# Attention with a mixture of experts on one core: the expert slot in another order, and the key copies of the first half between the exponentials

## The chip, the core and the metric

The kernel runs on one core of a Trainium2 chip. The core has a matrix engine (TensorE, PE in the rows; its weight loads are PEld), VectorE (DVE), ScalarE (ACT), GpSimd (POOL) and SyncE (SP), which here only issues DMAs. Each engine works through its own list of instructions in order and waits on semaphores that the others raise. The metric is the device time of one execution in microseconds, the median of the runs.

## What is computed

The input is 16 sequences of 512 rows with 128 features, 8192 rows in all. The rows are normalised, and three things are added: the row itself, the output of an attention block, and that of a layer of experts.

```
xn   = layernorm(x)
# attention, 16 heads of 64
h    = rmsnorm(xn) * norm_scale
q, k, v = h @ wq, h @ wk, h @ wv
w    = softmax(q k^T / 8)          # 512 x 512 for each sequence and head
a    = (w v) @ w_out + b_out
# experts: 8, of which each row uses 2
logit = silu(xn @ rw1 + rb1) @ rw2 + rb2
p, e  = softmax(top2(logit)), index
f     = sum over the 2 experts:  p * (silu(xn @ w1[e] + b1[e]) @ w2[e] + b2[e])
out  = x + a + f
```

## The kernel before

**Attention in ticks.** The attention is 64 units: a unit is one sequence, one half of its queries (256) and four pairs of heads. A unit has four ticks, `G` counts them from 0 to 255, and `k = G % 4` is the tick's place in its unit. In every tick PE makes two steps of scores (L313) into the two first pairs of PSUM banks, DVE takes the maxima of both (L555), ACT makes the exponentials (`PR`, L911) and DVE turns them (`PT`, L563). In ticks with k = 0 and 1 PE also multiplies the weights of the previous unit with the values (L332). At k = 2 DVE divides by the denominators (`OT`, L572), PE makes the queries of the next unit (L298) and the output projection (L345), and DVE adds the projection to `acc` (L595 or L598) after its second transpose. At k = 3 PE makes keys (L283 to L286) and values (L271), and ACT copies them to SBUF (`KS` L884, `V` L918). A new group of keys is needed first by the tick after one with G % 8 = 7.

**Two halves.** In ticks 0 to 127 the router also runs: it decides for each row the two experts and scatters the rows to a table in HBM that is sorted by expert. From tick 139 on the experts run, in 39 blocks of 512 rows (`NT`).

**The expert slot.** `SLOTS` holds the tick of each block: every tick with k = 2 from 142 on (29 of them), and every twelfth from 139 on, which has k = 3 (139, 151, 163 and so on to 247, ten of them). So nine slots with k = 3 follow right behind one with k = 2, and 20 with k = 2 stand alone. In the slot of block i, behind the attention's work of that tick, stand in the order of the list `PLAN[G]`: the *turn* of the rows of block i+1 (PE transposes them, L239 of `XG`; ACT and DVE split them into a high and a low part `X2`, L983 and L800), the *second product* of block i-1 (`expert_out`, PE L472; DVE scales and adds the bias, `give_back`, L813 and L817, to `YS`), and the *first product* of block i in four quarters (`expert_in`, PE L222 to L224). For each quarter ACT makes tanh (`ZT`, L995) and a biased copy (`HH`, L997), which frees the quarter's PSUM bank, and DVE multiplies the two (`halves`, L806). Quarters 0 and 1 of `halves` stand in the slot, quarters 2 and 3 in the next tick behind its maxima (the list `LATE`). Every engine reads the same `PLAN`, so an order in it is an order on PE, ACT and DVE alike. `give_back` ends in four indirect DMAs that POOL issues (`back`, L1174).

**PSUM banks.** Banks 0 to 3 hold scores. Banks 4 to 7 go around as a ring (`Ring`): each new product takes the next, and before it writes waits until the previous user of that bank has been read (`came_free`). The ring starts at bank 4 in each tick with k = 2. For a slot at such a tick the output projection's bank is the one just before the slot's first bank, and it is free when DVE has made `acc`.

**Key copies.** ACT's exponentials of a tick are two calls of `probs`. `alone(G)` says whether both copies of keys stand between them. Before, it holds in the second half alone, for ticks with G % 8 = 7 without a slot; in the first half one copy stands between them and one behind.

## Time and profile before

| | |
|---|---|
| median of 3 runs | 1888.17 us (1884.29 to 1891.51) |
| profiled execution | 1887.85 us, span 1886.0 us |
| PE busy | 1817.7 us, 96% of the span |
| DVE busy | 1625.3 us, 86% |
| ACT busy | 1209.1 us, 64% |
| granted TensorE clock | 0.997 |
| DMA | 130.15 MB, mean 69 GB/s |

The span is from the first instruction to the last of the profiled execution. A busy share says how long an engine had an instruction under way, not that it limits the kernel: each engine waits at some place of a tick for another, and the tick's length is set by the chain of such waits. The length of a tick is read as the distance between the first maxima (L555) of that tick and of the next. A row of a window has its limits, its length, then the busy time of PE, PEld, DVE, ACT and POOL in it (with the number of instructions), the granted TensorE clock, the busy share of the DMA engines and GB/s.

### The profile page before, as it was taken

To read this page: it belongs to the slowest core of one execution; us is meant where nothing else is said; L and a number is where in the kernel's file an instruction comes from. 1 tells how busy PE (TensorE), PEld (TensorE's weight loads), DVE (VectorE), ACT (ScalarE), POOL (GpSimd) and SP (SyncE) were. 2 spreads that over 40 slices of the span, in tenths; PEclk is the share of its full clock that TensorE was granted. 3 is DMA by queue.
4 is the path that set the end of the run, shared out by engine and by line. 5 is a ranking of instruction groups with operands and counts; after the bars stand their busy time and mean duration, and the time that the engine had idled before them with its cause. 6 is when DMAs were issued, how large, how long until landed. Compare 5 with 4: busy or idle time off the path is not lost.

```text
span 1886.0 us, 74660 instructions
## 1 busy us (share of the span) xinstructions
PE 1817.7 (96%) x32554; PEld 1177.0 (62%) x32554; DVE 1625.3 (86%) x2297; ACT 1209.1 (64%) x2987; POOL 733.0 (39%) x641
## 2 busy tenths in 40 slices
PE   8999999999999999998999999999999999999997
PEld 5555555555555555554567766767676667666765
DVE  6999999999999999989888888788888888888886
ACT  6666776666666666664666675666676666666663
POOL 4244655444544445432023334324324333333143
PEclk9999999999999999999999999999999999999999
DMA  3033321111111111111433434333433333333333
GB/s 96 22 83 109 101 95 52 42 48 37 48 37 48 48 48 46 30 40 56 110 74 78 90 73 90 78 84 78 89 74 66 92 65 87 76 84 78 79 74 56
DMA packets 154487, 130.15 MB, mean 69 GB/s; under 512 B 27664, under 2 KB 139024, under 8 KB 154128
## 3 DMA queue, kind: packets, MB, share of 16 engines
q1 hardware_dynamic: 123568, 104.65, 20.3%
q0 software_dynamic: 30592, 20.73, 8.1%
q8 instruction: 255, 4.18, 0.9%
q14 instruction: 72, 0.59, 0.1%
HBM read 93.15 MB, written 34.27 MB: 68 GB/s over the span
## 4 chain that ended last, share of the span: by engine, by line
PE 40%; ACT 28%; DVE 18%; issue 12%; DMA 1%; POOL 0%; POOLq 0%; SPq 0%; ACTq 0%; DVEq 0%
ACT PR L911 18%; PE pair L332 11%; DVE NM L555 8%; PE pair L472 8%; PE pair L313 7%; DVE PT L563 4%; PE pair L345 3%; ACT ZT L995 3%; ACT HH L997 3%; PE pair L298 3%; DVE OT L572 3%; ACT KS L884 1%; PE pair L239 1%; PE pair L388 1%; PE pair L271 1%
## 5 line engine op out<-in xcount | busy, mean ns | idle before, releaser
L911 ACT ACTIVATE PR<-pair,NM 128x512 f32<-128x512 f32 x1024 | 696.3, 697 | 536.9 <-DVE NM L555 536.4
L563 DVE STREAM_TRANSPOSE PT<-PR 128x1024 f32<-128x1024 f32 x512 | 633.2, 1241 | 119.2 <-ACT PR L911 105.7
L555 DVE TENSOR_REDUCE NM<-pair 128x2 f32<-128x1024 f32 x512 | 598.0, 1208 | 19.6 <-PE pair L313 18.9
L313 PE MATMUL pair<-KS,QS 64*32 64x512 f32 x8192 | 505.3, 598 | 16.6 <-ACT PR L911 9.3
L332 PE MATMUL pair<-PT,V 32*64 32x256 f32 x16384 | 479.7, 378 | 17.9 <-ACT HH L997 9.7
L332 PEld LDWEIGHTS pair<-PT,V 32*64 32x64 f32 x16384 | 383.6, 131 | 166.6 <-issue 107.3
L1174 POOL DMA_INDIRECT out<-YS,IDW x156 | 248.4, 1592 | 536.8 <-DVE YS L817 334.3
L313 PEld LDWEIGHTS pair<-KS,QS 64*32 64x32 f32 x8192 | 122.7, 106 | 261.7 <-issue 157.4
L911 ACT ACTIVATION_READ_ACCUMULATOR PR<-pair,NM 128x1 f32 x1024 | 218.9, 214 | 0.0
L995 ACT ACTIVATE ZT<-pair,BT 128x512 f32<-128x512 f32 x156 | 109.8, 704 | 108.1 <-PE pair L224 108.0
L1132 POOL DMA_INDIRECT slots<-XR,IDX x128 | 124.4, 972 | 73.9 <-issue 38.5
L472 PE MATMUL pair<-E,HH 128*128 128x128 f32 x1248 | 148.1, 277 | 2.9 <-DVE HH L806 2.9
L472 PEld LDWEIGHTS pair<-E,HH 128*128 128x128 f32 x1248 | 144.1, 194 | 4.4 <-DVE HH L806 3.8
L806 DVE SCALAR_TENSOR_TENSOR HH<-ZT,HH 128x512 f32<-128x512 f32 x156 | 104.1, 688 | 43.6 <-ACT HH L997 43.6
L298 PE MATMUL pair<-HF,WQ 128*128 128x256 f32 x512 | 126.1, 389 | 10.1 <-DVE OT L572 9.3
L298 PEld LDWEIGHTS pair<-HF,WQ 128*128 128x128 f32 x512 | 92.1, 190 | 62.2 <-DVE OT L572 49.5
L1121 POOL TENSOR_TENSOR TH<-TH,HS 128x512 f32<-128x512 f32 x64 | 82.1, 1282 | 120.1 <-ACT HS L951 120.1
L345 PE MATMUL pair<-OT,WO 128*128 128x256 f32 x512 | 123.6, 384 | 2.2 <-DVE OT L572 2.2
L271 PE MATMUL pair<-WV,HF 128*32 128x128 f32 x4096 | 125.1, 274 | 0.0
L271 PEld LDWEIGHTS pair<-WV,HF 128*32 128x32 f32 x4096 | 107.8, 110 | 23.4 <-issue 23.3
L345 PEld LDWEIGHTS pair<-OT,WO 128*128 128x128 f32 x512 | 94.7, 190 | 37.7 <-issue 9.5
L997 ACT ACTIVATE HH<-pair,BT 128x512 f32<-128x512 f32 x156 | 110.4, 708 | 0.0
(129 smaller groups left out, 1798.1 us busy)
## 6 DMA issues: line engine op xcount, KB each, us to landing
RB<-l_rows SPq DMA_DIRECT2D x128, 256.0 KB, 4.3
E<-w_tab SPq DMA_DIRECT2D x39, 512.0 KB
XG<-slots SPq DMA_DIRECT2D x39, 264.0 KB, 4.0
E<-in_w SPq DMA_DIRECT2D x39, 256.0 KB, 3.9
xin<-in_x SPq DMA_DIRECT2D x16, 256.0 KB, 2.8
XQ<-in_x SPq DMA_DIRECT2D x16, 256.0 KB, 3.1
l_rows<-RT SPq DMA_DIRECT2D x256, 2.0 KB
w_tab<-SPL SPq DMA_DIRECT2D x8, 512.0 KB, 2.6
```

Source lines behind the costliest of these rows:

```text
L271: m = pe.do.matmul(bank[bk][32 * a:32 * a + 32, j * P:j * P + P], HF[:, keys], WV[:, pair], start=True, stop=True, tile_position=(0, 32 * a))
L298: m = pe.do.matmul(bank[bk][:, 256 * i:256 * i + 256], WQ[:, pair], HF[:, 256 * half:256 * half + 256], start=True, stop=True)
L313: m = pe.do.matmul(bank[2 * (s % 2) + r][32 * c:32 * c + 32, :], QS[rows, u % 2, c, at:at + 32], KS[rows, g % 2, c, :], start=True, stop=T ...
L332: m = pe.do.matmul(bank[GH + a][DH * c:DH * c + DH, 0:256], V4[rows, g % 2, k, DH * c:DH * c + DH], moving, start=(k == 0), stop=(k == 15) ...
L345: m = pe.do.matmul(bank[bk][:, 0:256], WO[:, GH * (u // 2 % 2) + a, :], OT[:, a, :], start=(a == 0), stop=(a == GH - 1))
L472: m = pe.do.matmul(bank[bk][:, t * P:(t + 1) * P], HH[:, i % 2, c, t * P:(t + 1) * P], E2[:, i % 2, c * P:(c + 1) * P], start=(c == 0), st ...
L555: dve.do.tensor_reduce(NM[:, step % 4], pairs[s % 2][:], AX.X, ALU.max, negate=True).then_inc(sem["dve_max"])
L563: dve.do.transpose(PT[:].rearrange("p c k q -> p (c k) q")[:, :, 32 * slot:32 * slot + 32], PR[:, step % PRB].rearrange("p r k -> p (r k)" ...
L911: act.do.activation(PR[:, step % PRB, r, :], bank[2 * (s % 2) + r], ACT.Exp, bias=NM[:, step % 4, r:r + 1], accum_out=RS[:, g % 2, r, at:a ...
L995: act.do.activation(ZT[:, n % 2], ps, ACT.Tanh, bias=BT[:, i % 3, 8 + c:9 + c], scale=0.5).then_inc(sem["act_zt"])
L997: act.do.activation(HH[:, i % 2, c], ps, ACT.Identity, bias=BT[:, i % 3, c:c + 1]).then_inc(sem["act_zz"])
L1174: pool.do.indirect_dma_start(out, bass.IndirectOffsetOnAxis(ap=IDW[:, i % 4, t, 0:1].bitcast(U32), axis=0), YS[:, i % 2, t, :], None, comp ...
```

## The change

In `PLAN` a slot now holds the first product's four quarters, then the turn of the next block's rows, then the second product of the block before and its `back`. All four quarters of `halves` stand in the slot, and `LATE` is gone. `alone` holds for every tick with G % 8 = 7 that has no slot, so in the 16 such ticks of the first half both copies of keys stand between the two calls of `probs`; in the second half the places of the key copies are the same as before.

```diff
--- before.py
+++ after.py
@@ -191,17 +191,13 @@
 
         SLOTS = sorted([FIRST + 12 * k for k in range(NT - (UNITS - FIRST // 4 - 1))] + [4 * u + 2 for u in range(FIRST // 4 + 1, UNITS)])
         PLAN = {G: [] for G in range(TIMES + 8)}
-        LATE = {G: [] for G in range(TIMES + 8)}
         PLAN[FIRST - 1].append((0, "turn"))
         for i, G in enumerate(SLOTS):
+            PLAN[G] += [(i, "h", c) for c in range(NC)]
             if i + 1 < NT:
                 PLAN[G].append((i + 1, "turn"))
             if i:
-                PLAN[G].append((i - 1, "y"))
-            PLAN[G] += [(i, "h", c) for c in range(NC)]
-            LATE[G + 1] += [(i, c) for c in (2, 3)]
-            if i:
-                PLAN[G].append((i - 1, "back"))
+                PLAN[G] += [(i - 1, "y"), (i - 1, "back")]
         PLAN[TIMES - 1].append((NT - 1, "y"))
         PLAN[TIMES].append((NT - 1, "back"))
 
@@ -825,7 +821,7 @@
                         rows_low(i)
                     if what == "y":
                         give_back(i)
-                    if what == "h" and c[0] < 2:
+                    if what == "h":
                         halves(i, c[0])
 
             dve.do.memset(junk[:], 0.5).then_inc(sem["dve_junk"])
@@ -850,8 +846,6 @@
                     maxima(u, 2 * k + 1)
                 attending(G)
                 between(G)
-                for i, c in LATE[G]:
-                    halves(i, c)
                 if u < UNITS:
                     turn_probs(u, 2 * k)
                     if G % 8 == 2 and 0 < G // 8 <= NB:
@@ -895,7 +889,7 @@
                 act.do.copy(XT[:], bank[BANK["xT", r]]).then_inc(sem["act_xTs"])
 
             def alone(G):
-                return G >= 8 * NB and G % 8 == 7 and G not in SLOTS
+                return G % 8 == 7 and G not in SLOTS
 
             def probs(g, s):
                 step = STEPS * g + s
@@ -928,7 +922,7 @@
                 u, k = divmod(G, 4)
                 g, first = u // 2 + 1, u % 2 * 2
                 if k == 3 and g < 2 * NB:
-                    if G >= 8 * NB and not alone(G):
+                    if G in SLOTS or G % 8 == 3 and G >= 8 * NB:
                         keys(g, first)
                     if not alone(G):
                         keys(g, first + 1)
```

On PE, the slot of tick 194 before (from the projection's last matmuls on; `XG` are the rows that are turned, `E2,HH` the second product, `X2,E1` the first product, in brackets the semaphores waited for):

```order
L345 MATMUL pair3<-OT,WO 128x256 x3
L239 MATMUL pair3<-idn,XG 128x128 [waits s_rows_1]
L239 MATMUL pair3<-idn,XG 128x128 x3
L472 MATMUL pair2<-E2,HH 128x128 [waits s_act_q,s_e2_1,s_dve_s]
L472 MATMUL pair2<-E2,HH 128x128 x15
L222 MATMUL pair2<-X2,E1 128x512 [waits s_act_q,s_e1_0]
L223 MATMUL pair2<-X2,E1 128x512
L224 MATMUL pair2<-X2,E1 128x512
L222 MATMUL pair3<-X2,E1 128x512 [waits s_dve_acc]
```

And of the same slot of the changed kernel its last part, from the fourth quarter of the first product on (quarters one to three stand ahead of it, behind the projection, and wait for `s_e1_0` and `s_act_q`):

```order
L218 MATMUL pair3<-X2,E1 128x512 [waits s_dve_acc]
L219 MATMUL pair3<-X2,E1 128x512
L220 MATMUL pair3<-X2,E1 128x512
L235 MATMUL pair3<-idn,XG 128x128 [waits s_act_zz,s_rows_1]
L235 MATMUL pair3<-idn,XG 128x128 x3
L468 MATMUL pair2<-E2,HH 128x128 [waits s_act_zz,s_e2_1,s_dve_s]
L468 MATMUL pair2<-E2,HH 128x128 x15
L309 MATMUL pair0<-KS,QS 32x512 [waits s_act_exp]
```

The wait for `acc` was at the second quarter, after turn and second product; it is now at the fourth, ahead of both, and the second product is the slot's last work on PE. The lines are four lower because the diff takes lines away.

On DVE, the same slot and the tick after it, before (`HH<-ZT,HH` are the quarters, `X<-pair,X` the turn's low part, `NM` the maxima):

```order
L598 TENSOR_TENSOR acc<-pair,acc 128x256
L800 TENSOR_TENSOR X<-pair,X 128x512
L813 SCALAR_TENSOR_TENSOR YS<-pair,B 128x512
L817 TENSOR_TENSOR YS<-YS,IDW 128x512
L806 SCALAR_TENSOR_TENSOR HH<-ZT,HH 128x512 x2
L555 TENSOR_REDUCE NM<-pair 128x2 x2
L806 SCALAR_TENSOR_TENSOR HH<-ZT,HH 128x512 x2
L563 STREAM_TRANSPOSE PT<-PR 128x32x32 x2
```

And there in the changed kernel:

```order
L594 TENSOR_TENSOR acc<-pair,acc 128x256
L802 SCALAR_TENSOR_TENSOR HH<-ZT,HH 128x512 x4
L796 TENSOR_TENSOR X<-pair,X 128x512
L809 SCALAR_TENSOR_TENSOR YS<-pair,B 128x512
L813 TENSOR_TENSOR YS<-YS,IDW 128x512
L551 TENSOR_REDUCE NM<-pair 128x2 x2
L559 STREAM_TRANSPOSE PT<-PR 128x32x32 x2
```

All four quarters now stand ahead of the next tick's maxima, and so do, right before them, the two operations on the second product.

On ACT, a tick of the first half with G % 8 = 7 before:

```order
L911 ACTIVATE PR,RS<-pair,NM 128x512 x2
L884 COPY KS<-pair 128x512
L911 ACTIVATE PR,RS<-pair,NM 128x512 x2
L884 COPY KS<-pair 128x512
L918 COPY V<-pair 128x512 x2
L895 COPY XT<-pair 128x512
```

And the same tick of the changed kernel:

```order
L905 ACTIVATE PR,RS<-pair,NM 128x512 x2
L878 COPY KS<-pair 128x512 x2
L905 ACTIVATE PR,RS<-pair,NM 128x512 x2
L912 COPY V<-pair 128x512 x2
L889 COPY XT<-pair 128x512
```

The second copy of keys has moved from behind the tick's last exponentials to ahead of them.

## Rows read from the trace of the kernel before

**Rows 1.** The page: the chain that ended last, by engine

```profile
PE 40%; ACT 28%; DVE 18%; issue 12%; DMA 1%; POOL 0%; POOLq 0%; SPq 0%; ACTq 0%; DVEq 0%
```

**Rows 2.** Waits: who waited for whom, us in total, times, longest

```profile
ACT ZT L995 <- PE pair L224: 108.0, 38, 3.7
```

**Rows 3.** Timeline of DVE, tick 194: start, length, instruction, [idle before, releaser]

```profile
1366.91 2.34 DVE L555 TENSOR_REDUCE NM<-pair 128x2 f32<-128x1024 f32 x2
...
1373.11 0.39 DVE L598 TENSOR_TENSOR acc<-pair,acc 128x256 f32<-128x256 f32 x1
...
1374.21 0.69 DVE L813 SCALAR_TENSOR_TENSOR YS<-pair,B 128x512 f32<-128x512 f32 x1
...
1378.09 2.35 DVE L555 TENSOR_REDUCE NM<-pair 128x2 f32<-128x1024 f32 x2
1380.36 1.28 DVE L806 SCALAR_TENSOR_TENSOR HH<-ZT,HH 128x512 f32<-128x512 f32 x2
```

**Rows 4.** Timeline of PE, tick 194

```profile
1370.00 0.60 PE L239 MATMUL pair<-idn,XG 128*128 128x128 f32 x4
1370.44 3.74 PE L472 MATMUL pair<-E,HH 128*128 128x128 f32 x32
1373.93 0.48 PE L222 MATMUL pair<-X,E 128*128 128x512 f32 x1
...
1376.89 1.95 PE L313 MATMUL pair<-KS,QS 64*32 64x512 f32 x32
```

**Rows 5.** Timeline of ACT, tick 194: first and last of the eight on the quarters

```profile
1374.91 0.69 ACT L995 ACTIVATE ZT<-pair,BT 128x512 f32<-128x512 f32 x1 [2.52 <-PE pair L224]
...
1378.91 0.73 ACT L997 ACTIVATE HH<-pair,BT 128x512 f32<-128x512 f32 x1
```

**Rows 6.** Windows of ticks 186, 190, 195, 191, 135, 187 and 188

```profile
1299.47:1311.07 11.60, 11.60 (x92) 9.62 (x98) 9.07 (x12) 7.93 (x18) 3.26 (x4) 1.00 0.09 24
1337.11:1348.54 11.43, 11.43 (x88) 9.44 (x95) 8.48 (x11) 7.43 (x17) 6.42 (x5) 1.00 0.68 146
1378.09:1384.23 6.14, 6.10 (x118) 3.22 (x102) 6.11 (x10) 6.14 (x15) 4.80 (x4) 1.00 0.41 37
1348.54:1355.32 6.78, 6.58 (x126) 3.34 (x118) 6.22 (x9) 6.16 (x15) 5.68 (x4) 1.00 0.33 31
900.88:907.47 6.59, 5.49 (x110) 2.89 (x116) 5.10 (x8) 4.72 (x12) 0.00 (x0) 1.00 0.93 209
1311.07:1324.52 13.45, 12.81 (x166) 9.39 (x150) 9.60 (x15) 10.23 (x23) 4.77 (x4) 1.00 0.48 105
1324.52:1330.69 6.17, 5.22 (x160) 3.74 (x160) 5.79 (x8) 3.97 (x11) 0.00 (x0) 1.00 0.03 5
```

**Rows 7.** Window of tick 192, which has no expert work

```profile
1384.23:1389.43 5.20, 5.07 (x160) 3.75 (x160) 4.72 (x5) 2.82 (x9) 0.00 (x0) 1.00 0.11 18
```

**Rows 8.** Timeline, first half, ticks 84 to 90: DVE, ACT and PE

```profile
569.44 2.36 DVE L555 TENSOR_REDUCE NM<-pair 128x2 f32<-128x1024 f32 x2 [0.52 <-PE pair L313]
...
586.98 1.25 DVE L563 STREAM_TRANSPOSE PT<-PR 128x1024 f32<-128x1024 f32 x1 [0.58 <-ACT PR L911]
...
586.82 0.60 ACT L884 COPY KS<-pair 128x512 f32<-128x512 f32 x1
587.29 1.11 ACT L918 COPY V<-pair 128x512 f32<-128x512 f32 x2
...
587.48 1.95 PE L313 MATMUL pair<-KS,QS 64*32 64x512 f32 x32 [0.20 <-ACT KS L884]
...
600.88 1.99 PE L298 MATMUL pair<-HF,WQ 128*128 128x256 f32 x8 [0.41 <-DVE OT L572]
```

**Rows 9.** Granted clock and idle PE: tick 139, the last tick, its second product

```profile
930.87 0.63 PE L239 MATMUL pair<-idn,XG 128*128 128x128 f32 x4 [1.81 <-ACT KS L884]
...
1863.54 5.46 PE L472 MATMUL pair<-E,HH 128*128 128x128 f32 x32 [2.86 <-DVE HH L806]
...
1863.50:1869.00 5.50, 5.46 (x32) 5.27 (x32) 2.61 (x4) 0.67 (x3) 1.55 (x1) 0.69 0.28 25
```

## The prediction, made before the changed kernel was run

> **What bounds the kernel now.** I read the chain that ended last first: it changes between three engines, PE 40%, ACT 28%, DVE 18% [rows 1], so no engine is the limit by itself and the time has to be worked out tick by tick. The list of waits then names what looks wasteful in a slot: ACT waits 108.0 us in all for the first product, 38 times, 2.8 us each [rows 2]. The windows show what kinds of tick there are. A tick without expert work takes 5.20 us with DVE busy for 4.72 and PE for 5.07 [rows 7]; slots at k = 2 take 11.43 and 11.60 [rows 6] and, by its two first maxima, tick 194 takes 1378.09 - 1366.91 = 11.18 [rows 3]. The timelines of DVE, PE and ACT in tick 194 show the slot's own chain. PE ends the second product and goes over to the first at 1373.93, hands over the first quarter, and ACT, which was free 2.52 us earlier, starts at 1374.91 [rows 4, 5]. DVE multiplies two quarters and is at the next maxima at 1378.09 [rows 3]. The bound of a slot is thus PE until its first quarter, then ACT, then DVE. What matters in the changed order is which of these the next maxima stand behind.
>
> **The slot at k = 2, 29 times.** Nothing is computed more or less; it is all order. After the projection PE is at the slot's work at 1370.00, 3.09 us after the first maxima of the tick [rows 3, 4]. Now the first product comes first. It takes 1376.89 - 1373.93 = 2.96 us, 0.74 a quarter [rows 4]. Its banks go on in the ring from the projection's: the fourth quarter has the projection's own bank and waits for DVE's `acc`, as the order's wait says. `acc` stands behind DVE's second transpose, which the change doesn't touch, and ends at 1373.11 + 0.39 = 1373.50, 6.59 us into the tick [rows 3]. Without that wait the quarter would start at 3.09 + 3 x 0.74 = 5.31; so PE stands idle for 1.3 us. Before, it used this bank after turn and second product, when `acc` was long made.
>
> From there on the chain has no gap: 0.06 us for the semaphore (an estimate: from DVE's first `OT`, half of a pair, to PE's start at 600.88 it is no more [rows 8]), 0.74 for the quarter, 1370.44 - 1370.00 = 0.44 for the turn, and from the second product's start to DVE's read of it 1374.21 - 1370.44 = 3.77 [rows 3, 4]. The two waits for ACT's reads of quarters one and two don't bind: ACT was free at 1374.91 - 2.52 = 1372.39 even behind the turn's copy of 0.6, so its first quarter starts at about 4.9 us; it needs (1378.91 + 0.57 - 1374.91) / 4 = 1.14 us for each [rows 5] and has read the second at 7.2, while PE gets to the second product at 6.59 + 0.06 + 0.74 + 0.44 = 7.83. Then DVE has `give_back`, two operations of 0.69 [rows 3], and only behind them the next maxima. Sum: 7.83 + 3.77 + 1.38 = 12.98, say 13.0. Against tick 194 that is +1.8, against 190 +1.55, against 186 +1.4 [rows 3, 6]. The fourth kind (G % 16 = 6) is put with 186. The mean is 1.54; ticks that were already longer for reasons of their own lose less, so I take 1.5. The last slot, tick 254, is counted with the end; 28 x 1.5 = +42.0 us.
>
> How low could it be? If `acc` came so early that PE didn't wait, the second product would still wait for ACT's second quarter (7.2), so 7.2 + 3.77 + 1.38 = 12.35. And ACT and DVE alone give no less: four quarters end on ACT at 4.9 + 4.56 = 9.5, DVE's fourth at 10.2, its low part after the turn at 10.9, `give_back` 12.3. Below: 28 x (12.35 - 11.46) = +25. ACT's wait of 2.8 us does go, but all that ACT gains stays in front of DVE's in-order queue, which now waits for PE's last work in the slot.
>
> **The tick after a slot.** It gives back the two quarters of `halves`, 1.28 us on DVE between maxima and transposes [rows 3]. Where tick k = 3 is G % 8 = 3 and no slot, DVE filled it (6.11 of 6.14 busy [rows 6]). Without the quarters it is like a bare tick, 5.20, with 0.4 for the denominators at the unit's end (an estimate: 6.14 less maxima of 2.3, quarters of 1.2 and two transposes of 1.15 [rows 3, 6, 8]): 5.6, so -0.55, not -1.28, because DVE then waits for the exponentials. Ten times: -5.5. Where G % 8 = 7, ACT sets the length: 6.78 in tick 191 against 6.59 in tick 135, the same work without a slot before it [rows 6], so -0.2, ten times: -2.0.
>
> **The slot at k = 3, nine times behind another and once, tick 139, by itself.** Its first quarter's bank is that of a key copy. ACT starts half a pair of maxima into the tick, 1.2, and has 4.72 of exponentials and copies, as in tick 135 [rows 3, 6]; that makes 5.9. Its second quarter is read at 5.9 + 2 x 1.14 + 0.1 = 8.3; PE's second product starts there and is read at 8.3 + 3.77 = 12.1, `give_back` ends at 13.4, and 0.4 of denominators make 13.85. Before: 13.45 [rows 6]. So +0.4, and the tick after goes from 6.17 to a bare 5.20 [rows 6, 7], -0.97. Together 9 x -0.57 = -5.1. Tick 139 has no second product before it and now waits for four quarters and the turn instead of two: about +2.2 - 0.96 = +1.2.
>
> **The key copy of the first half, 16 ticks.** The copy takes 587.29 - 586.82 = 0.47 us of ACT [rows 8]. Moved ahead of the tick's last exponentials it delays these, and DVE already waited 0.58 for them before its transpose at 586.98. In return PE loses a wait of 0.20 for the copy at 587.48. Who is late next? DVE's chain runs on from here until PE waits 0.41 for its `OT` at 600.88, and DVE in turn waits for PE at the tick after a k = 3 (0.52 at 569.44) [rows 8]. So the transpose is on the path and PE's 0.20 is not: 16 x 0.47 = +7.5. If PE were the path it would be -3; I keep both ends and take +7.5, since the waits on either side name DVE.
>
> **The end.** In the last tick the second product waited 2.86 us for the late quarters [rows 9]; now it does not. DVE reads it behind its transposes in any case, so this gives back tick 254's own loss of about 2.4 and some more: -1 for both.
>
> **DMA and POOL.** SP and POOL have the same list as before. Rows and weights for the next block are fetched in the slot ahead, `YS` is ready later by 5 us, and POOL has no work close behind it. Nothing.
>
> **Sum.** 42.0 - 5.5 - 2.0 - 5.1 + 1.2 + 7.5 - 1.0 = +37.1. The profiled execution took 1887.85 us, its span 1886.0; the median of the runs, 1888.17, is 0.3 above it. 1887.85 + 37.1 = 1924.95, so 1925.
>
> **The clock.** Tick 139 shows PE idle for 1.81 us with the granted clock at 1.00 in the ticks around it [rows 6, 9]; the idle of 2.86 us before the last second product was followed by 0.69, between the levels of 1.2 and 2.4 GHz, and 5.46 us for it instead of 3.74 [rows 4, 9]. The new wait is 1.3 us, so I cost it at nothing. The Trainium skill speaks against this: "TensorE: Matmul & The Clock Gate", section "A second HAM failure mode: psum-queue depth-cycling", tells of a kernel whose PE, going through PSUM banks in turn, had small idle gaps between groups and swung between the two clocks. By that rule the time would be that of the third rival below; the trace, with waits for banks of up to 1.81 us at 1.00, does not agree so far.
>
> **Rivals.**
> 1. *No wait for `acc`.* Another reader of the bank order could say that DVE's `acc` will come earlier once DVE has no late quarters. For it: the queue before `acc` is shorter only in ticks at k = 3. Against it: `acc` follows the second transpose of its own tick, which ACT sets. Slot 12.35: 1888 + 37 - 28 x 0.65 = 1907. Chance 0.07.
> 2. *PE is the bound and has no new wait: not slower.* Place: the fourth quarter. For it: PE is busy for 5.07 of 5.20 in a bare tick [rows 7], so ticks behind a slot could repay a late start if PE ran ahead. Then DVE's 1.5 would vanish, and PE's waits around the slots at k = 3 would go (13.45 - 12.81 = 0.64 and 6.17 - 5.22 = 0.95 [rows 6], nine times -14), with +7.5 from the first half: 1888 - 7 = 1881. It decides if PE waits under 0.3 us for the fourth quarter. Against it: DVE reaches each next maxima last in rows 3. Chance 0.03.
> 3. *The clock falls in the slots.* 1.7 us more for the second product in 28 slots, +48: 1972. Chance 0.04.
> 4. *The change is only half of this:* the key copy costs nothing or gains 3: 1914 to 1917. That lies inside my range and has no chance of its own.
>
> **Numbers.** The forecast of 1925, with its own range of 1912 to 1934, has 0.83; rival 1 0.07, rival 2 0.03, rival 3 0.04, and 0.03 remain for a time within the noise. The range of 1908 to 1937 leaves out rival 2, rival 3 and part of rival 1. About 0.5% is what a measurement of this kernel can tell from no change. Faster by more than that 0.02, within it 0.04, slower 0.94.
>
> **What would show it.** Ticks at k = 2 with a slot of about 13.0 us, the last wait in them DVE's for the second product (L809, from PE L468); a PE wait of 1.3 us for `acc` before the fourth quarter (L218 from DVE L594 or L591), 28 times; ACT's wait for PE before ZT gone; ticks behind lone slots of 5.6 and 6.6; 7.8 in the first half where 7.3 was. I am wrong if slots at k = 2 stay under 12 us, or if the ticks without expert work change.

## The result and the profile after

| | before | changed |
|---|---|---|
| median of 4 runs | 1889.25 us (1884.29 to 1891.51) | 1939.08 us (1938.28 to 1940.4) |
| profiled execution, span | 1887.85, 1886.0 us | 1938.28, 1936.5 us |
| PE busy, DVE busy, ACT busy | 1817.7, 1625.3, 1209.1 us | 1830.9, 1644.2, 1208.8 us |
| granted TensorE clock | 0.997 | 0.997 |

The changed kernel is slower: 1.0268 times the time before, with an interval of 1.0246 to 1.029. The forecast was 1925 with a range up to 1937, so the direction held and the size did not: +50 where +37 was forecast. Beside e1 to e8 the kernel before took about 1888 us; in e9 to e15 every kernel, the one before too, took some 8% longer (the last section shows where in the tick order), and those are compared among themselves, or in ticks that are the same in both.

The page, the chain that ended last by engine; DVE has gone from 18% to 30% of it, and PE from 40% to 20% [rows 1]:

```profile
ACT 32%; DVE 30%; PE 20%; issue 15%; DMA 2%; POOL 0%; SPq 0%; POOLq 0%; ACTq 0%; DVEq 0%
```

The waits of the changed kernel (us in total, times, longest):

```profile
PE pair L218 <- DVE acc L594: 18.6, 15, 1.4
...
PE pair L218 <- DVE acc L591: 12.4, 14, 1.3
...
ACT ZT L989 <- DVE HH L802: 2.5, 4, 1.1
```

PE now waits for `acc` 15 + 14 = 29 times, once in each slot at k = 2. ACT's 108.0 us behind the first product [rows 2] are gone.

The slot of tick 178 (first maxima 1264.54) on DVE, then on PE, then on ACT: start, length, instruction, [idle before, releaser]:

```profile
1264.54 2.34 DVE L551 TENSOR_REDUCE NM<-pair 128x2 f32<-128x1024 f32 x2
...
1270.74 0.39 DVE L594 TENSOR_TENSOR acc<-pair,acc 128x256 f32<-128x256 f32 x1
...
1274.34 0.69 DVE L802 SCALAR_TENSOR_TENSOR HH<-ZT,HH 128x512 f32<-128x512 f32 x1 [0.46 <-ACT HH L991]
...
1276.20 0.69 DVE L809 SCALAR_TENSOR_TENSOR YS<-pair,B 128x512 f32<-128x512 f32 x1 [0.57 <-PE pair L468]
1276.92 0.69 DVE L813 TENSOR_TENSOR YS<-YS,IDW 128x512 f32<-128x512 f32 x1
1277.53 2.35 DVE L551 TENSOR_REDUCE NM<-pair 128x2 f32<-128x1024 f32 x2
```

```profile
1271.18 0.50 PE L218 MATMUL pair<-X,E 128*128 128x512 f32 x1 [1.29 <-DVE acc L594]
...
1272.42 3.74 PE L468 MATMUL pair<-E,HH 128*128 128x128 f32 x32
```

```profile
1269.40 0.72 ACT L989 ACTIVATE ZT<-pair,BT 128x512 f32<-128x512 f32 x1
...
1278.79 0.69 ACT L905 ACTIVATE PR<-pair,NM 128x512 f32<-128x512 f32 x1 [4.07 <-DVE NM L551]
```

Set against [rows 3 to 5]: ACT starts the quarters 4.86 us into the tick instead of 8.00, and then stands idle for 4.07 us before the next exponentials. PE stands 1.29 us at the fourth quarter, its second product starts at 7.88, DVE reads it at 11.66 and is at the next maxima at 12.99. The chain of the prediction is in these rows link by link.

Windows of ticks 186, 187, 188 and 195 of the changed kernel (columns as in [rows 6]), and of tick 175:

```profile
1326.08:1339.24 13.16, 12.25 (x100) 9.74 (x98) 10.43 (x15) 9.37 (x20) 1.92 (x2) 1.00 0.13 29
1339.24:1353.28 14.04, 13.06 (x166) 9.56 (x150) 9.89 (x15) 9.83 (x21) 6.69 (x5) 1.00 0.45 102
1353.28:1358.48 5.20, 5.20 (x168) 3.35 (x160) 4.72 (x6) 2.78 (x8) 0.00 (x0) 1.00 0.03 5
1408.99:1414.61 5.62, 5.62 (x118) 3.22 (x102) 5.11 (x8) 4.37 (x12) 4.65 (x3) 1.00 0.27 26
1237.81:1252.96 15.15, 14.06 (x199) 10.49 (x191) 11.91 (x14) 10.05 (x21) 8.84 (x7) 1.00 0.44 94
```

They were 11.60, 13.45, 6.17 and 6.14 [rows 6]; tick 175 was 13.44. In the first half, tick 87 of the changed kernel, ACT and then DVE and PE, where [rows 8] have the copy of keys at the transpose:

```profile
594.55 0.71 ACT L905 ACTIVATE PR<-pair,NM 128x512 f32<-128x512 f32 x1
...
595.22 1.10 ACT L912 COPY V<-pair 128x512 f32<-128x512 f32 x2
```

```profile
595.39 1.25 DVE L559 STREAM_TRANSPOSE PT<-PR 128x1024 f32<-128x1024 f32 x1 [1.07 <-ACT PR L905]
```

```profile
595.14 1.95 PE L309 MATMUL pair<-KS,QS 64*32 64x512 f32 x32
```

DVE's wait for the exponentials has grown from 0.58 to 1.07, and PE's 0.20 for the copy is gone. The tick is 7.80 instead of 7.32.

**All ticks, sorted by kind**, each measured from first maxima to first maxima in the two profiled executions:

| ticks | count | before | after | difference in sum | forecast |
|---|---|---|---|---|---|
| slots at k = 2, without 254 | 28 | 11.56 | 13.02 | +42.36 | +42.0 |
| after lone slots, G % 8 = 3 | 10 | 6.14 | 5.62 | -5.24 | -5.5 |
| after lone slots, G % 8 = 7 (the tenth is tick 255, counted with the end) | 9 | 6.79 | 6.59 | -1.80 | -2.0 |
| slots at k = 3 and the ticks after | 9 + 9 | 13.44, 6.17 | 14.04 (two 15.15), 5.20 | -1.7 | -5.1 |
| tick 139 and the one after | 2 | 9.92, 6.17 | 12.32, 5.20 | +1.4 | +1.2 |
| first half, G % 8 = 7 | 16 | 7.32 | 7.80 | +7.52 | +7.5 |
| first half, all others | 112 | 6.42 | 6.42 | +5.97 | 0 |
| tick 254 and all behind it | | 9.60 | 11.58 | +2.9 | -1.0 |
| the rest and the start | | | | -1.0 | 0 |

Before and after are medians. The sum is +50.5, as the spans say. What the forecast missed is +6.0 in ticks of the first half that the change doesn't touch, +3.9 at the end and +3.4 at the slots with k = 3.

**Where VectorE stands still.** The extra time of the first half lies in four ticks: 33 (+2.09), 34 (+1.28), 41 (+0.99) and 90 (+2.37), together 6.7; small differences in the others take 0.8 off. In three of the four a VectorE operation is much longer than usual; tick 34 has another cause, shown further down. Tick 33 of the changed kernel, on DVE and on POOL:

```profile
233.61 2.64 DVE L669 SCALAR_TENSOR_TENSOR gt<-gt,CON 128x32 f32<-128x32 f32 x1
```

```profile
233.91 1.29 POOL L1153 TENSOR_TENSOR SPL<-RAW,SPL 128x512 fp32r<-128x512 f32 x1
235.15 1.04 POOL L1059 TENSOR_TENSOR HR<-xin,mv 128x512 f32<-128x512 f32 x1
236.27 1.04 POOL L1062 TENSOR_TENSOR HR<-HR,sqo 128x512 f32<-128x512 f32 x1
```

An operation on 128 x 32 elements took 2.64 us, where the same line takes 0.17 in other ticks, and it ended at 236.25, 0.06 us behind the second of two GpSimd operations. In tick 175 the quarters of `halves` do the same, DVE and then POOL:

```profile
1245.05 4.21 DVE L802 SCALAR_TENSOR_TENSOR HH<-ZT,HH 128x512 f32<-128x512 f32 x3 [1.93 <-ACT HH L991]
```

```profile
1244.91 1.64 POOL L1059 TENSOR_TENSOR HR<-xin,mv 128x512 f32<-128x512 f32 x1
1246.62 1.38 POOL L1062 TENSOR_TENSOR HR<-HR,sqo 128x512 f32<-128x512 f32 x1
```

Taken apart, the first quarter lasts 2.05 us and the second 1.52 instead of 0.69. Over the whole profiled execution, ten DVE operations were over 0.4 us longer than the median of their line, 12.4 us beyond it in all, and GpSimd had a TENSOR_TENSOR under way beside each; before, there were two such, 2.3 us beyond it, both in tick 127.

**Tick 34.** No operation on VectorE is stretched in it. PE, which had waited for the stretched chain of tick 33, ran its next products at a lower granted clock (PE, then the window):

```profile
239.38 3.04 PE L294 MATMUL pair<-HF,WQ 128*128 128x256 f32 x8 [2.55 <-DVE OT L568]
```

```profile
239.40:242.20 2.80, 2.80 (x8) 2.30 (x9) 2.80 (x4) 1.11 (x3) 0.00 (x0) 0.64 0.00 0
```

In e1, which has the same stretched operation in tick 33, PE waits 2.40 us there, the clock stays at 1.00, the same eight matmuls take 1.99 us and tick 34 is 6.51 as before. So +1.28 of the +6.0 is the clock's. That it fell because of the longer wait is likely and not shown.

**The end.** POOL's first and last additions of the last two blocks, before:

```profile
1857.76 1.55 POOL L1174 DMA_INDIRECT out<-YS,IDW  x1 [16.12 <-DVE YS L817]
...
1876.47 1.55 POOL L1174 DMA_INDIRECT out<-YS,IDW  x1 [0.30 <-issue]
```

And in the changed kernel, with the last product of PE and DVE's last operation:

```profile
1909.87 1.55 POOL L1168 DMA_INDIRECT out<-YS,IDW  x1 [21.62 <-DVE YS L813]
...
1926.99 1.55 POOL L1168 DMA_INDIRECT out<-YS,IDW  x1 [0.30 <-issue]
```

```profile
1909.94 3.84 PE L468 MATMUL pair<-E,HH 128*128 128x128 f32 x32
1915.94 8.85 PE L328 MATMUL pair<-PT,V 32*64 32x256 f32 x256 [2.15 <-DVE YS L809]
```

```profile
1933.03 0.69 DVE L611 TENSOR_TENSOR xin<-pair,xin 128x512 f32<-128x512 f32 x1 [4.25 <-DMA xin<-out]
```

The last second product is no longer late (3.84 us and no wait, against 5.46 and 2.86 [rows 9]). But counted from the last tick's first maxima (1859.93 and 1909.51) the last addition starts at 17.48 instead of 16.54 us, and the end waits for the output that is read behind these additions. The chain that ended last, in order of time (start, length, step), says what the second group of additions waited for:

```profile
1915.42 4.51 DMA out<-YS,IDW
```

VectorE had the last `YS` ready at 1916.52, but the second group starts only at 1921.44, behind the landing of the first group's last addition. Before, the second group started at 1870.92, 0.46 us behind `YS`. The order moved the first group: it starts 0.36 us behind the last tick's first maxima, and before 2.17 us ahead of them.

### The profile page after: what moved, and what is told of

The parts are those of the page before. It is cut to its first block, busy times and chain, and to the rows that moved or that the text cites. A ratio compares the mean times of both kernels' runs of the same rounds, so it can differ in the third digit from the quotient of the medians.

```text
span 1936.5 us, 74661 instructions
## 1 busy us (share of the span) xinstructions
PE 1830.9 (95%) x32554; PEld 1179.4 (61%) x32554; DVE 1644.2 (85%) x2297; ACT 1208.8 (62%) x2987; POOL 734.2 (38%) x641
## 4 chain that ended last, share of the span: by engine, by line
ACT 32%; DVE 30%; PE 20%; issue 15%; DMA 2%; POOL 0%; SPq 0%; POOLq 0%; ACTq 0%; DVEq 0%
ACT PR L905 24%; DVE NM L551 13%; PE pair L468 7%; DVE PT L559 6%; PE pair L328 4%; DVE OT L568 4%; PE pair L309 3%; ACT QS L884 3%; ACT KS L878 2%; PE pair L384 1%; DVE YS L809 1%; ACT ZT L989 1%; ACT HH L991 1%; DVE YS L813 1%; ACT V L912 1%
## 5 line engine op out<-in xcount | busy, mean ns | idle before, releaser
L309 PE MATMUL pair<-KS,QS 64*32 64x512 f32 x8192 | 510.8, 597 | 19.4 <-ACT PR L905 16.7
L905 ACT ACTIVATION_READ_ACCUMULATOR PR<-pair,NM 128x1 f32 x1024 | 211.5, 207 | 0.0
L802 DVE SCALAR_TENSOR_TENSOR HH<-ZT,HH 128x512 f32<-128x512 f32 x156 | 111.8, 718 | 69.6 <-ACT HH L991 68.6
```

Of the source, the lines that this page charges most:

```text
L309: m = pe.do.matmul(bank[2 * (s % 2) + r][32 * c:32 * c + 32, :], QS[rows, u % 2, c, at:at + 32], KS[rows, g % 2, c, :], start=True, stop=T ...
L905: act.do.activation(PR[:, step % PRB, r, :], bank[2 * (s % 2) + r], ACT.Exp, bias=NM[:, step % 4, r:r + 1], accum_out=RS[:, g % 2, r, at:a ...
```

## The experiments

### e1_keys: the key copies alone

```diff
-                return G >= 8 * NB and G % 8 == 7 and G not in SLOTS
+                return G % 8 == 7 and G not in SLOTS
-                    if G >= 8 * NB and not alone(G):
+                    if G in SLOTS or G % 8 == 3 and G >= 8 * NB:
```

> Only the key copy of the first half is moved; the expert slots are as before. My theory: the 16 ticks with G % 8 = 7 take 7.8 us instead of 7.32 (the copy's 0.47 delays the exponentials, and DVE's transposes behind them), nothing else changes in them: 1889 + 7.5 = 1897. The changed kernel's first half had 6 us more than that, in ticks 33, 34, 41 and 90, where a tiny DVE operation took 1 to 2.6 us while POOL computed. If these come of the shifted times, they stand in this run too and it takes 1903; if they are chance, they are gone or elsewhere. Rival (PE was the path and loses its 0.2 us wait for the copy): 1886.

1897.76 us, ratio 1.0053 (1.0039 to 1.0067). The 16 ticks are 7.80, +7.50 together, and ticks 33 and 41 have their +2.09 and +1.00 again, with the same stretched operations. So this half costs 9.4 us: the copy itself, and collisions that it causes by moving everything behind it. Tick 34 is 6.51 and tick 90 is 7.21 here, as before: of the changed kernel's four long ticks, two (3.1 us) are seen in this second trace and two (3.6 us) in the changed kernel's alone.

### e2_slot: the slots alone

The changed kernel with `alone` as before.

> Only the slot is changed (order and quarters), the key copies are as before. My theory: the second half is tick by tick that of the changed kernel (slots at k = 2 13.0, slots at k = 3 14.0, two of them 15.1 if POOL meets DVE's quarters in the same places), the first half that of before: 1939 less 7.5 to 13.5, so 1926 to 1932. Rival (the two edits share a cost): under 1920.

1928.11 us, ratio 1.0209 (1.0194 to 1.0225). The slots at k = 2 give +42.50, those at k = 3 are 14.04 and in ticks 175 and 223 again 15.15. +39.8 and +9.4 make 49.2 of the 49.8: within the scatter of the runs the two halves add.

### e3_order and e4_quarters: the order alone, the quarters alone

e3 has the new `PLAN` and keeps `LATE`; e4 has the old `PLAN` and all four quarters in the slot:

```diff
-            LATE[G + 1] += [(i, c) for c in (2, 3)]
-                    if what == "h" and c[0] < 2:
+                    if what == "h":
```

> The slot in the new order, but quarters 2 and 3 on DVE stay in the next tick; key copies as before. My theory (the next maxima stand behind the second product's read, whatever DVE does before it): slots at k = 2 stay at 13.0 although two quarters have left them, and the ticks after a slot keep 6.14, 6.79 and 6.17, so it loses the 17 us that the quarters' place gave back: 1929 + 17 = 1946. Rival (the four quarters ahead of the maxima are the cost, the order is free or a gain): slots back near 11.5, in all 1885 to 1895.

> The old order of the slot, but all four quarters stand ahead of the next tick's maxima; key copies as before. My theory: the old order starts ACT's quarters 3.1 us later, so here the maxima wait for the fourth instead of the second quarter, 2 x 1.14 = 2.3 us: slots at k = 2 13.4 to 13.9, slots at k = 3 15.7, ticks after a slot 5.6, 6.6 and 5.2: 38 x 2.3 - 17 = +70, so 1959, worse than both edits together (1929). The two edits are then not additive: 1946 and 1959 alone, 1929 together. Rival (additive): order + quarters = slot.

e3 1934.97 us, ratio 1.025 (1.0235 to 1.0266): slots at k = 2 are 13.01, and the ticks behind lone ones take 6.15 and 6.59, those behind k = 3 5.72. e4 1968.34, ratio 1.0425 (1.0408 to 1.0441): slots at k = 2 are 13.69, at k = 3 17.15. The loss of the slot is thus that of the order. To have all quarters in it costs nothing there and gives back 0.5 us in the ticks behind it with G % 8 = 3 or behind k = 3; the 0.2 in those with G % 8 = 7 is the order's. Without the order the quarters cost more than the whole change, because they come last on DVE (e4, tick 194, the last quarter and the next maxima):

```profile
1414.62 0.69 DVE L805 SCALAR_TENSOR_TENSOR HH<-ZT,HH 128x512 f32<-128x512 f32 x1 [0.46 <-ACT HH L996]
1415.23 1.22 DVE L554 TENSOR_REDUCE NM<-pair 128x2 f32<-128x1024 f32 x1
```

The two edits don't add, as e4's expectation said: in the new order the quarters lie beside PE's second product. The totals missed by 11 us below and 9 us above. In e3 the place of the quarters is worth about 10 us and not 17 (see the ticks behind the slots). In e4 the slots at k = 3 take 17.15 and not 15.7, and that is the clock. Tick 187, PE, then a window in it:

```profile
1346.19 1.09 PE L238 MATMUL pair<-idn,XG 128*128 128x128 f32 x4 [2.69 <-ACT KS L883]
```

```profile
1346.10:1349.50 3.40, 3.31 (x16) 3.34 (x17) 1.44 (x2) 1.90 (x4) 0.00 (x0) 0.50 0.06 8
```

PE waits 2.7 us in each of the nine slots, for the copy of keys that frees the bank. In eight of them the granted clock then falls to 0.50 for a while and the slot takes 17.0 to 17.2; in tick 163 it stays at 1.00 behind the same wait, and the slot takes 15.56.

### e5_acc: acc ahead of the second transpose

e2 with the projection's addition one step earlier on DVE in slots:

```diff
+                    if k == 2 and G in SLOTS:
+                        project_out(u - 1)
-                if k == 2 and 0 < u <= UNITS:
+                if k == 2 and 0 < u <= UNITS and G not in SLOTS:
```

> The slot of the changed kernel with key copies as before (1928.1), and in slots at k = 2 DVE makes acc ahead of its second transpose, in the gap of 1.07 us in which it waits for the exponentials. My theory (PE waits 1.3 us for acc before the fourth quarter and the chain from there is without a gap): that wait goes, the second product next waits for ACT to read the second quarter, 7.3 us into the tick, and slots at k = 2 take 7.3 + 3.8 + 1.4 = 12.5 instead of 13.0: 28 x -0.55 = -15, so 1913. It also prices the wait: 1.3 us of idle PE is worth 0.55 of time. Rival (the wait for acc is the whole loss of the slot): 11.7 us, 1891. Rival (DVE's queue sets the slot, not PE): 13.0 still, 1928.

1918.62 us, ratio 1.0163 (1.0147 to 1.0178), 9.5 less than e2. Slots at k = 2 are 12.65 in 22 of 28. PE no longer waits for `acc` (tick 194, PE, first maxima 1380.11):

```profile
1385.75 0.39 PE L220 MATMUL pair<-X,E 128*128 128x512 f32 x1
1386.41 0.63 PE L235 MATMUL pair<-idn,XG 128*128 128x128 f32 x4 [0.28 <-ACT HH L993]
1387.57 3.70 PE L468 MATMUL pair<-E,HH 128*128 128x128 f32 x31 [0.53 <-ACT HH L993]
```

The wait for ACT takes its place, as forecast for this case (12.35; 12.5 in the expectation). So `acc` is the bound in these 22, and worth only 0.3 to 0.4 us of the 1.46 by which the slot grew. The six slots with G % 16 = 10 keep their 13.16: there the second product starts at 7.98 us without the wait for `acc` and at 7.97 with it (tick 186), since ACT frees its bank that late in either kernel. Over all 28 slots the gain is 8.1 us, where 15 were expected.

### e7_lateback: the second product read behind the next maxima

e2 with `give_back` moved on DVE to behind the next tick's maxima.

> The slot of the changed kernel with key copies as before (1928.1), and DVE reads the second product (both operations of give_back) behind the next tick's maxima instead of ahead of them. My theory (the maxima stand behind DVE's read of PE's last product): the maxima then wait only for PE's next scores, which stand behind that product: slots at k = 2 take 7.85 + 3.5 + 1.0 = 12.4, slots at k = 3 12.9; the tick after pays for the read, 6.1 to 6.6. Sum -15 - 10 + 5 + 9 = -11 or -12, so 1916: most of the loss stays, since PE's order keeps the next scores late. Rival (only DVE's order is at fault): slots at k = 2 fall to 11.5, 1890.

1956.7 us, ratio 1.0357 (1.0339 to 1.0376), where 1916 was expected. The slots did get shorter (12.77 and 13.38), but the ticks behind k = 3 take 7.94 to 10.8 instead of 5.2. Tick 188, PE and DVE:

```profile
1352.52 3.71 PE L328 MATMUL pair<-PT,V 32*64 32x256 f32 x128 [2.35 <-DVE YS L809]
```

```profile
1357.36 1.23 DVE L551 TENSOR_REDUCE NM<-pair 128x2 f32<-128x1024 f32 x1 [1.98 <-PE pair L309]
```

PE needs the second product's bank for the values of the next tick, and DVE waits for PE at the maxima behind it. In both places tried something waits for `give_back`: in the changed order PE ends the second product too late for either. I had not asked who needs the bank.

### e6_gate: GpSimd's normalisation behind the maxima

e2 with GpSimd's normalisation of rows, from shortly before the second half on, kept back until DVE's first maxima of its tick:

```diff
+                    if b >= EARLY:
+                        pool.wait_ge(sem["dve_max"], 2 * G + 1)
```

> The slot of the changed kernel with key copies as before (1928.1), and POOL's two large operations on the next sequence's rows (HR) wait, from tick 129 on, for the first maxima of their own tick, so that they can't run ahead into DVE's quarters in ticks 175 and 223. My theory (DVE's operation stands still while POOL's runs beside it): both ticks fall from 15.15 to 14.04, DVE's quarters in them from 2.05 and 1.52 to 0.69 us; -2.2 us, 1926. Rival (the indirect DMAs or the fetches beside them slow the quarters): they stay at 15.15.

One run, 1921.97 us, span 1920.2 against e2's 1927.1. Ticks 175 and 223 are 14.05 instead of 15.15, and tick 127 is 7.35 instead of 9.64, which had the two stretched operations of the kernel before. No DVE operation was stretched any more. The last of four indirect DMAs in tick 175 on POOL, and the second quarter, which had taken 1.52:

```profile
1228.62 1.56 POOL L1170 DMA_INDIRECT out<-YS,IDW  x1 [0.30 <-issue]
```

```profile
1231.06 0.69 DVE L802 SCALAR_TENSOR_TENSOR HH<-ZT,HH 128x512 f32<-128x512 f32 x1 [0.47 <-ACT HH L991]
```

The indirect DMA still stands beside the first quarter (1229.90, 0.69 us), so the rival falls. With this the two GpSimd operations on `HR` are shown as the cause of the two longer slots: they moved away, their amount unchanged, and the 2.2 us came back. The whole run is 6 us under e2's median; 2.3 more are tick 127, the rest is not explained, and it is one run.

### e10_apart and e13_two: the same for the first half

e1 with one wait more on GpSimd ahead of the subtraction (`SPL`), in every tick that has one (e10), and only in ticks 33 and 41 (e13):

```diff
+                    pool.wait_ge(sem["dve_tr"], 2 * G + 3)
```

```diff
+                    if G in (33, 41):
+                        pool.wait_ge(sem["dve_gate"], 15 * (G // 8 - 1) + 11)
```

> The key copies alone (1897.8 us, ticks 33 and 41 longer by 2.1 and 1.0 us than before), and POOL's subtraction for the expert weights' low part (SPL, eight times between ticks 26 and 40) waits until DVE has made the first transpose of the tick after the one it is written in. My theory (the shifted times bring DVE's tiny operation of ticks 33 and 41 beside POOL's subtraction, and it stands still until that ends): ticks 33 and 41 are back at 6.4, the 16 ticks stay at 7.80, in all 1894.7. Rival (the two ticks are long through the DMAs): they stay at 8.5 and 7.4.

> The kernel before with the key copies of the first half moved, and one wait more: in ticks 33 and 41 GpSimd's subtraction on the split weights (SPL) waits until VectorE has made its small code operation of that tick (L673), the one that stood stretched to 2.64 and 1.55 us beside it. Theory (the small operation stands still because of GpSimd's): tick 33 is 2.1 us and tick 41 1.0 us shorter than with the key copies alone, no small operation is longer than 0.3 us there, the other ticks stay, the time is about 3 us under that of the key copies alone. Rival (the stretch comes from something else, a late semaphore or the scatters under way on the same DMA queues): both operations stay stretched and both ticks stay as they were.

e10 2060.62 us beside 2040.39 for the kernel before: a miss. Ticks 27, 28, 31, 35, 36 and 39 grew by 1.3 to 5.4 us against the kernels beside it, and twelve operations were stretched that had not been, in other lines and ticks (27, 31, 35, 39), each beside a GpSimd TENSOR_TENSOR. What stands behind the waiting subtraction in GpSimd's list came later: the router's first multiplication of tick 27 at 213.33, and at 208.83 in e13. e13 2037.83 beside 2043.22, ticks 33 and 41 both 6.42, and no stretched operation in it. But in e9 to e15 ticks 32 and 40 take 9 to 11 us more in every kernel, which moves what runs beside what, and e15, without any of these waits, also has 6.42 in both. With the key copies and without the waits no kernel ran there. So neither tells the theory from its rival. The collisions of the first half are read from the traces (ticks 33 and 41: the same operations, the same ends, in two kernels; tick 90 in one), and not shown by taking them away.

### e14_waits: the changed kernel with both waits

> The changed kernel with two waits more on GpSimd: that one in ticks 33 and 41, and, for the normalisation of rows in the second half, one for VectorE's first maxima of the tick. Theory (the part of the loss that the prediction left out is VectorE standing still beside GpSimd): ticks 33, 41, 175 and 223 lose 2.1, 1.0, 1.1 and 1.1 us, tick 127 loses about 2, in all 6 to 8 us less than the changed kernel, so about 1.7 to 2.1% over the kernel before on the same chip; k = 2 slots stay at 13.0, k = 3 slots are 14.04 all. Rival (the slot at k = 3 is longer by itself, or the waits of GpSimd delay what VectorE needs from it): the time stays within 2 us of the changed kernel's.

2070.57 us beside 2043.22, and 2071.96 for e15. The slots of ticks 175 and 223 are 14.11, those of e15, without the waits, 15.16 and 15.14; no operation was stretched. That repeats e6. The ratio is 1.013 where 1.017 to 1.021 was expected, one run each. It can't be set against the changed kernel, which has no run beside these; and in e9 to e15 the old order's slots at k = 2 take 11.7 to 11.8 us and not 11.56, the new order's 13.02 as ever, so the order costs about 11 us less in them there.

### e11_end and e15_end: the last slot in the old order

One kernel, run twice: e2 with the second product ahead in the last slot, and its quarters 2 and 3 late.

> The slot of the changed kernel with key copies as before (1928.1), but the last slot, tick 254, in the old order and with its late quarters. My theory (the end is set by POOL's two groups of indirect adds, which begin when the last but one second product is read, and the new order reads it 4.5 us later in its tick): tick 254 falls from 11.58 to 9.6 and the tail behind the last maxima from +0.7 to 0 against before; -2.7, so 1925.4. Rival (the tail comes from the late quarters that keep the last product waiting, as my prediction had it, so the old order makes the end slower): 1929 or more.

> The changed slots, key copies as before, and the last slot (tick 254) in the old order with its two late quarters. Theory of the end (the loss there is the last slot's own new length plus GpSimd's later start with the last blocks' additions): tick 254 9.8 instead of 11.6 and the time behind the last maxima up by 0.2 instead of 0.8 us, as in an earlier run of this kernel; in all 2 to 2.5 us under the changed slots alone. Rival (the end is bound by the transfers of the last block whatever the order): tick 254 shrinks and the part behind the last maxima grows by as much.

2070.29 and 2071.96 us. Tick 254 is 9.80 and 9.83 instead of 11.58, so the growth of tick 254 is the order's. What lies behind it was +0.15 against the kernel before in one run and +0.93 in the other, and among e9 to e15 it varies as much between kernels with the old end (e12 +1.18, e13 +0.17), so these two runs don't settle the +0.88. The earlier traces say more. From the last tick's first maxima to the end the old slot takes 25.95 to 26.42 us (the kernel before, e1, e8) and the changed one 26.81 to 26.97 (the changed kernel, e2, e5, e6). And e4, with the old order but the quarters ahead, takes 24.82, -1.27: there `YS` is ready as early as in the changed kernel (7.01 us behind the last tick's first maxima, and 10.53 before), the first group of additions starts 4.45 us ahead of those maxima, and the second at once. In e3 the first group is as late as in the changed kernel, but its last addition lands in 3.15 us and not 4.51, and the whole takes 25.86. By these rows the late first group takes the gain away, and the longer landing (4.3 to 4.5 us in the four kernels with the changed end) makes the loss; why it is longer stays open.

### e12_gate: the wait of e6 in the kernel before

> The kernel before with nothing but POOL's two operations on the next sequence's rows held back from tick 129 on. My theory: tick 127 7.3 instead of 9.64, no DVE operation longer than its kind's median by over 0.4 us; -2.3, 1885.6. Rival: no change, 1887.9.

2039.41 us beside 2040.39 (2034.75 to 2044.82): no difference that one run can show. Its trace has no stretched operation, but tick 127 takes 12.37 us there, so the 7.3 of the expectation can't be tried.

### e8_hybrid and e9_both: the new order where it costs least

The kernel before, with the new order and all quarters only in the nine slots at k = 3 that follow another; e9 adds the wait of e6.

```diff
+            ahead = G % 4 == 3 and G > FIRST
+            if ahead:
+                PLAN[G] += [(i, "h", c) for c in range(NC)]
...
+            if not ahead:
+                PLAN[G] += [(i, "h", c) for c in range(NC)]
+                LATE[G + 1] += [(i, c) for c in (2, 3)]
```

> The kernel before, with the new slot order and all four quarters in nine slots only: those at k = 3 behind another slot, where the change cost 0.6 us and gave back 0.97 in the tick after. All others, and the key copies, as before. My theory: 9 x (0.6 - 0.97) = -3.3 us, 1885, at the edge of what five rounds can tell; by the profile nine ticks of 14.04 and 5.20 instead of 13.44 and 6.17, if POOL doesn't meet the quarters (nothing before these slots is later than in the kernel before). Rival (the gain in the tick after needs the new order in the slot ahead as well): nothing gained, 1888 to 1890.

> The kernel before with two changes: the new slot order in the nine slots at k = 3 behind another slot (1883.6 by itself), and POOL's two operations on the next sequence's rows held back, from tick 129 on, until the first maxima of their own tick. My theory (a DVE operation stands still while POOL's runs beside it, and in tick 127 this costs 2.3 us): tick 127 falls from 9.65 to 7.3, all else stays: 1881.3. Rival (tick 127 is long for another reason that hit the kernel with the wait by chance): 1883.6.

e8 1883.58 us (1881.17 to 1886.89, 11 runs) beside 1887.86: ratio 0.9979 (0.997 to 0.9988), a little faster than before. The nine slots are 14.24 (+7.22) and the ticks behind them 5.21 (-9.19 over nine). The slots were expected at 14.04. Tick 187, where DVE comes to the second product:

```profile
1320.26 0.69 DVE L817 SCALAR_TENSOR_TENSOR YS<-pair,B 128x512 f32<-128x512 f32 x1 [0.28 <-PE pair L476]
```

That accounts for 2.0 of the 4 us; the slots at k = 2, which it leaves alone, were 2.3 us shorter in the sum. e9 2036.02 (12 runs) beside 2040.39, ratio 0.998 (0.9969 to 0.9991), the same as e8's: the wait adds nothing that can be measured. The 2.3 us that were expected of tick 127 can't be tried there, since that tick takes over 12 us in all of e9 to e15 but one (11.99).

## Why the prediction was half right

- **The slot at k = 2**: right, 13.02 for 13.0, and for the reason given. 29 waits of up to 1.4 us for `acc`, then turn, second product, `give_back` on one chain (tick 178). e5 takes the wait away and gets 12.65 in 22 slots where the lower end said 12.35; in the other six ACT is as late as `acc`, which the prediction had ruled out for all. e3 shows that the order alone does it.
- **The tick after, lone slots**: right, 5.62 and 6.59 for 5.6 and 6.6.
- **The key copy**: right, 7.80 and +7.52. DVE's wait took on the copy's length, and PE's 0.20 was worth nothing.
- **The clock**: right for the slots, where it stayed at 1.00 with 29 idle times of up to 1.4 us on PE, so the third rival did not come true. But the reason was thin, and part of that is luck. It set 1.3 us against the 1.81 us of tick 139, behind which the clock stayed up; in the same trace PE waits 1.72 us in tick 128 and then has a granted clock of 0.50 (row in the last section). In the changed kernel the clock cost 1.3 us in tick 34, and in e4 eight slots swing between the two levels behind waits of 2.7 us for a bank. There the rule of the Trainium skill cited in the prediction agrees with the trace, and in the changed kernel's slots it does not.
- **The slot at k = 3**: direction right, size too small. 14.04 for 13.85 (seven of nine), since the second product is read at 12.28 and not 12.1; that is 9 x 0.19 = 1.7 us. Another 2.2 are ticks 175 and 223, and the ticks behind give back 0.5 more than forecast.
- **"DMA and POOL. Nothing."**: the step that failed. Its reason looked at GpSimd as a waiter for `YS` only. It had no term for GpSimd's own operations, which go by their own chain and met other DVE operations once DVE was displaced by half a microsecond. The measured price is 5.4 us in ticks 33, 41 and 90 and 2.2 in two slots, 7.6 of the 13.4 that were missing; the 1.3 of tick 34 is the clock's, right behind such a tick. The 2.2 are shown by e6 and e14. The 5.4 are read from traces (3.1 from two kernels, 2.4 from one), and no run takes them away. The trace of before held the warning, in its two stretched operations near 850 us (1.62 and 1.07 us for 0.19), and I had not looked for operations much longer than their line's median. The Trainium skill has the rule, in "SBUF — State Buffer", section "Who interferes with whom": a VectorE instruction with two SBUF inputs contends with a GpSimd instruction that reads SBUF, one with at most one SBUF input, outside the 2-port modes, does not. The rows agree as to which operations stretch (`gt<-gt,CON`, `HH<-ZT,HH`) and which don't (maxima from PSUM, transposes).
- **"The end. -1."**: failed by 3.9 us. The own loss of tick 254 was counted with 2.4 and is 1.98 (e11, e15). The gain set against it did not come: the wait of 2.86 us on PE went, and `YS` was ready 3.5 us earlier, but the second group of additions that GpSimd issues then waited for the landing of the first, which starts later in the new order. e4, without that, has a gain (-1.27 behind tick 254). So the step that failed is the path: I had followed the engine with the long wait and not the chain that ended last.
- **Rivals**: the first two (no wait for `acc`, PE as the bound) fall by the 29 waits, the third by the clock of 1.00 in the slots. The fourth (a free key copy) falls by e1.

## What to carry to other kernels

When an edit moves one engine's queue by a fraction of a microsecond in many places, list which operations of the other engines it will now meet: look in the trace of before for operations longer than the median of their line, and see what runs beside them. Work that an in-order engine must finish before the step that feeds all the others (here the maxima) should hold the product that is ready first, not the one that PE ends last. And for the end of a kernel follow the chain that ends it, not the longest wait near it.

## What the runs showed of the hardware

**A small VectorE operation took 2.64 us beside GpSimd.** The row of tick 33 starts 0.30 us ahead of GpSimd's first TENSOR_TENSOR and ends only with the second, 236.25 against 236.19; so the operation seemed to stand through two of them. By the same section of the Trainium skill the one that issues first gets the shared pair and the other blocks; the records, with 233.61 for VectorE and 233.91 for GpSimd, don't show that order, though the starts on POOL are rough. A copy with one SBUF input was hit too, in tick 90, behind an addition (the section names copies among the operations that can enter a 2-port mode); both take 0.17 us in other ticks:

```profile
615.38 1.25 DVE L691 TENSOR_TENSOR PM<-PM,gt 128x8 f32<-128x8 f32 x1
616.66 1.21 DVE L694 COPY PM<-PM 128x8 f32<-128x8 f32 x1
```

GpSimd's own operations were longer too beside the quarters, 1.64 and 1.38 us in tick 175, where the same two lines took 1.04 in tick 33.

**Idle time on PE and the clock.** 29 idle times of up to 1.4 us in slots left the granted clock at 1.00. For longer ones the length alone does not tell: behind 1.81 us (tick 139, before), 2.40 (tick 33, e1) and 2.7 (tick 163, e4) it stayed at 1.00, behind 1.72 (tick 128, before), 2.55 (tick 33, the changed kernel) and 2.7 (eight slots of e4) it fell to 0.50 for a time; here behind tick 128 of the kernel before:

```profile
857.90:861.20 3.30, 3.30 (x56) 1.36 (x48) 3.27 (x5) 1.29 (x4) 0.00 (x0) 0.50 0.65 156
```

Behind the wait of 2.15 us at the end of the changed kernel it was lower too:

```profile
1915.00:1925.00 10.00, 8.85 (x256) 8.02 (x256) 1.51 (x4) 0.00 (x0) 4.76 (x4) 0.83 0.45 76
```

**Gaps between single matmuls.** Of the 150 us that the kernels of e9 to e15 took longer, about 95 lie in twelve ticks of the first half with G % 8 = 7 (some 15 us instead of 7.3), and 7 to 11 in each of ticks 32, 40 and 132. In e13, tick 55, PE, then a window behind it:

```profile
425.26 0.33 PE L239 MATMUL pair<-idn,XR 128*128 128x128 f32 x1
426.47 0.27 PE L239 MATMUL pair<-idn,XR 128*128 128x128 f32 x1 [0.88 <-issue]
...
427.92 0.31 PE L239 MATMUL pair<-idn,XR 128*128 128x128 f32 x1 [0.46 <-issue]
```

```profile
430.00:434.28 4.28, 4.28 (x27) 1.19 (x30) 0.00 (x0) 1.07 (x2) 0.64 (x1) 0.50 0.54 138
```

PE makes single matmuls with gaps that no semaphore explains, and then runs at the lower clock level, 0.50. Why those gaps came up in these runs and not in the earlier ones was not tried and stays open.
